# A graph network's tensor product: when the second 0/1 tile and the second turned row of a two-block group are made

## The reference

```python
w = _mlp(emb, fc1_w1, fc1_w2)                 # per edge: 512 weights from 10 numbers
s_t = a1 * (einsum(s1, Wss) + einsum(vdot1, Wvv))
v_t = a1 * (einsum(s1, Wsv) * sh1 + einsum(v1, Wvs))
w2 = _mlp(emb, fc2_w1, fc2_w2)
scal, gates, vecs = ...                       # second product, of s_t and v_t in the same way
edge_out = concatenate([tanh(scal), vecs * tanh(gates)]) * norm
return segment_sum(edge_out, edge_dst, num_segments=12500)
```

## Time and profile before

| | |
|---|---|
| median of 3 runs | 30745.3 us (30692.2 to 30746.5) |
| profiled execution | 30631.3 us, span 30629.5 us |
| busy, whole span | PE 82%, PEld 53%, DVE 59%, ACT 15%, POOL 55% |
| tensor-product stage | from about 21011 us to 30600 us |
| its costliest VectorE groups | L1763 2308.7 us, L1755 2050.7 us |
| its costliest TensorE groups | L1894 3515.9 us, L1882 2122.7 us |

### The profile page before, as it was taken

How to read it: one execution, slowest core, us unless ns; L and a number is a source line. 1 busy time by engine, 2 the same in 40 slices (tenths; PEclk the granted TensorE clock), 3 DMA queues, 4 the chain that set the end, 5 groups by cost and what they waited for, 6 DMA issues and landing times. The chain is left out here.

```text
span 30629.5 us, 606961 instructions
## 1 busy us (share of the span) xinstructions
PE 25062.6 (82%) x149627; PEld 16349.8 (53%) x149628; DVE 18026.0 (59%) x47075; ACT 4486.4 (15%) x12240; POOL 16710.3 (55%) x16857
## 2 busy tenths in 40 slices
PE   8777776666669888876999997666888888888888
PEld 6444443222238888854767675663444444444444
DVE  9211114666663333334666666886777777777777
ACT  4111111111110000001111111221111111111111
POOL 0677776777767777734777775552333333333332
PEclk9555555555555555555566666997999999999999
DMA  2111112222221111103333336552222222222222
GB/s 65 35 30 30 30 30 47 51 51 51 51 44 25 25 25 25 25 13 54 79 80 79 79 79 90 172 171 68 70 70 70 70 71 71 71 69 70 69 70 64
DMA packets 2615643, 1869.03 MB, mean 61 GB/s; under 512 B 1600555, under 2 KB 2081065, under 8 KB 2613814
## 3 DMA queue, kind: packets, MB, share of 16 engines
q1 hardware_dynamic: 1914438, 1424.41, 17.5%
q0 software_dynamic: 516000, 217.22, 5.7%
q10 hardware_dynamic: 184400, 220.54, 2.9%
HBM read 1621.01 MB, written 238.82 MB: 61 GB/s over the span
## 5 line engine op out<-in xcount | busy, mean ns | idle before, releaser
L2030 POOL DMA_INDIRECT rows_x<-x_table,index x3125 | 3031.6, 970 | 6787.0 <-DMA index<-in_src 6025.1
L1295 POOL DMA_INDIRECT rows<-x_table,index x3625 | 3456.8, 954 | 1997.6 <-issue 1237.4
L162 PE MATMUL banks<-rows,onehot 128*128 128x33 f32 (+1 forms) x14440 | 3416.8, 413 | 1062.1 <-issue 601.7
L547 POOL DMA_INDIRECT rows<-x_table,index x3125 | 3026.0, 968 | 1852.1 <-issue 939.7
L162 PEld LDWEIGHTS banks<-rows,onehot 128*128 128x128 f32 x14440 | 3185.9, 328 | 1370.0 <-issue 1360.8
L905 POOL DMA_INDIRECT bucket_pairs<-pair,place_int x3125 | 3145.7, 1007 | 1275.2 <-issue 1213.5
L696 POOL DMA_INDIRECT rows<-x_table,index x3125 | 3108.0, 995 | 1019.5 <-issue 951.7
L1894 PE MATMUL banks<-first,same_unit 128*128 128x384 f32 (+1 forms) x10000 | 3515.9, 478 | 0.0
L1205 DVE CUSTOM_DVE_ANT_0 junk<-banks,mask 128x320 f32<-128x320 f32 x5800 | 2550.5, 486 | 1546.4 <-PE banks L1240 1523.9
L1763 DVE TENSOR_TENSOR second<-banks,h 128x384 f32<-128x384 f32 (+1 forms) x5000 | 2308.7, 484 | 1093.8 <-PE banks L1894 1050.6
L1882 PE MATMUL banks<-u_turned,w_tensor 32*128 32x384 f32 (+1 forms) x10000 | 2122.7, 502 | 522.7 <-DVE first L1755 522.7
(11 more groups left out here) (396 smaller groups left out, 38439.1 us busy)
## 6 DMA issues: line engine op xcount, KB each, us to landing
key_row<-key_rows SPq DMA_DIRECT2D x1450, 320.0 KB
h<-hidden_dram SPq DMA_DIRECT2D x10000, 40.0 KB
key_row<-dst_rows SPq DMA_DIRECT2D x625, 320.0 KB
rows<-x_table,index POOLq DMA_INDIRECT x9875
a_dram<-a ACTq DMA_DIRECT2D x625, 160.0 KB
a<-a_dram SPq DMA_DIRECT2D x625, 160.0 KB
rows_dram<-rows ACTq DMA_DIRECT2D x725, 90.0 KB
x_rows<-rows_dram SPq DMA_DIRECT2D x725, 90.0 KB
```

The source lines that it names most:

```text
L162: mm = nc.tensor.matmul(m["ps"][7][:, 0:width], m["onehot"][j % 3][:, t * P:(t + 1) * P], rows[:, t, :], start=t == 0, stop=t == T - 1)
L547: nc.gpsimd.indirect_dma_start(out=m["rows"][j][:, t * W:t * W + F], out_offset=None, in_=m["x_table"], in_offset=bass.IndirectOffsetOnAxi ...
L1295: nc.gpsimd.indirect_dma_start(out=m["rows"][j][:, t * XA:t * XA + F], out_offset=None, in_=m["x_table"], in_offset=bass.IndirectOffsetOnA ...
L2030: nc.gpsimd.indirect_dma_start(out=m["rows_x"][j][:, t * F:(t + 1) * F], out_offset=None, in_=m["x_table"], in_offset=bass.IndirectOffsetO ...
```

## The change

Three things move, and only for two-block groups do products and tiles themselves come in another order:

- On VectorE the first add of g-3 goes from behind the gates to between `first` quarter 1 and the front (`dve_first_visit`). It now waits for `returned` of group g-2 too. With two blocks, the second 0/1 tile is made right behind it. The second add stays where the visits were (`dve_further_visits`).
- The second turned row is made without a loop around it; the wait until TensorE has used it and the memset L1818 go behind `second` quarter 1 (`dve_turned_last`), which reads the group's word once more.
- The words are read at the start of VectorE's turn, since the first add needs a block number. On TensorE, further visits wait for `first_added` and `summed_up` and step a counter first.

A loop over third and later visits stays in the code for groups with more than two blocks, of which there are none.

```diff
-            with dve.Fori(1, visits) as k:
+            nc.vector.tensor_scalar(m["hot_turned"][:, :], m["key_row"][j][:, :], m["part_at"][:, 1:2], None, ALU.is_equal).then_inc(s["more_turned"], 1)
+
+    def dve_turned_last(dve, i, j, n):
+
+        with dve.If(n > 1):
+            _, visits, further = window_of(nc, dve, m, s, SLOTS * i + j)
+            with dve.If(visits > 2), dve.Fori(2, visits) as k:
                 dve.wait_ge(s["more_owned"], ONE + further + k - 1)
...
+    def dve_first_visit(dve, i, j, first, n):
+        g = SLOTS * i + j
+
+        if not (isinstance(i, int) and g == GROUPS - 1):
+            dve.wait_ge(s["returned"], ONE + g + 2)
         dve.wait_ge(s["first_summed"], ONE + g + 1)
-        add(sums_at(0), first).then_inc(s["first_added"], 1)
+        dve_add(sums_at(0), first).then_inc(s["first_added"], 1)
+        with dve.If(n > 1):
+            hot(g, j, 1).then_inc(s["more_hot"], 1)
+
+    def dve_further_visits(dve, i, j, n):
...
+            with dve.If(visits > 2), dve.Fori(2, visits) as k:
+                dve.wait_ge(s["summed"], ONE + further + k - 1)
+                add(sums_at(1), block_of_visit(k - 1)).then_inc(s["added"], 1)
                 hot(g, j, k).then_inc(s["more_hot"], 1)
-                dve.wait_ge(s["summed"], ONE + further + k)
-                add(sums_at(1), to).then_inc(s["added"], 1)
+            dve.wait_ge(s["summed"], ONE + further + visits - 1)
+            add(sums_at(1), block_of_visit(visits - 1)).then_inc(s["added"], 1)

     def dve_turn(dve, i, j):
+        if there(i, j, -3) or there(i, j, 2):
+            first, n, _, n_ahead = turn_words(dve, i, j)
         if there(i, j, 0):
             dve_first(dve, i, j, 0)
         if there(i, j, -1):
             dve_second(dve, *at(i, j, -1), 2)
         if there(i, j, 0):
             dve_first(dve, i, j, 1)
+        if there(i, j, -3):
+            dve_first_visit(dve, *at(i, j, -3), first, n)
         if there(i, j, 1):
             dve_front(dve, *at(i, j, 1))
         if there(i, j, -1):
             dve_second(dve, *at(i, j, -1), 3)
-        if there(i, j, -3) or there(i, j, 2):
-            first, n, _, n_ahead = turn_words(dve, i, j)
...
         if there(i, j, -3):
-            dve_visits(dve, *at(i, j, -3), first, n)
+            dve_further_visits(dve, *at(i, j, -3), n)
...
             dve_second(dve, i, j, 1)
+        if there(i, j, 2):
+            dve_turned_last(dve, *at(i, j, 2), n_ahead)
...
     def pe_further_visits(pe, i, j, n):
         with pe.If(n > 1):
             _, visits, further = window_of(nc, pe, m, s, SLOTS * i + j)
+            pe.wait_ge(s["first_added"], ONE + SLOTS * i + j + 1)
+            if not (isinstance(i, int) and SLOTS * i + j == GROUPS - 1):
+                pe.wait_ge(s["summed_up"], ONE + SLOTS * i + j + 2)
+            pe.sem_inc(s["going"], 1)
```

More of the change, by code:

```diff
@@ L1818, in dve_turned_further, with dve_add @@
         nc.vector.memset(m["done"][:, :], 0.0).then_inc(s["rows_owned"][j], 1)
-    def dve_visits(dve, i, j, first, n):
+    def dve_add(sums, to):
+        block = m["acc"][:, bass.ds(to * W, W)]
+        return nc.vector.tensor_tensor(block, block, sums, ALU.add)
+    def dve_first_visit(dve, i, j, first, n):
         g = SLOTS * i + j
-        def add(sums, to):
-            block = m["acc"][:, bass.ds(to * W, W)]
-            return nc.vector.tensor_tensor(block, block, sums, ALU.add)
+        if not (isinstance(i, int) and g == GROUPS - 1):
+            dve.wait_ge(s["returned"], ONE + g + 2)
         dve.wait_ge(s["first_summed"], ONE + g + 1)
-        add(sums_at(0), first).then_inc(s["first_added"], 1)
+        dve_add(sums_at(0), first).then_inc(s["first_added"], 1)
[3 more added lines that the diff above has]
+        g = SLOTS * i + j
+        add = dve_add
         with dve.If(n > 1):
             begin, visits, further = window_of(nc, dve, m, s, g)
-            with dve.Fori(1, visits) as k:
-                to = nc.s_assert_within(begin + k, 0, NB - 1, skip_runtime_bounds_check_because="first + n <= NB")
+            block_of_visit = lambda k: nc.s_assert_within(begin + k, 0, NB - 1, skip_runtime_bounds_check_because="first + n <= NB")
+            with dve.If(visits > 2), dve.Fori(2, visits) as k:
+                dve.wait_ge(s["summed"], ONE + further + k - 1)
+                add(sums_at(1), block_of_visit(k - 1)).then_inc(s["added"], 1)
                 hot(g, j, k).then_inc(s["more_hot"], 1)
-                dve.wait_ge(s["summed"], ONE + further + k)
-                add(sums_at(1), to).then_inc(s["added"], 1)
+            dve.wait_ge(s["summed"], ONE + further + visits - 1)
+            add(sums_at(1), block_of_visit(visits - 1)).then_inc(s["added"], 1)
     def dve_turn(dve, i, j):
+        if there(i, j, -3) or there(i, j, 2):
+            first, n, _, n_ahead = turn_words(dve, i, j)
         if there(i, j, 0):
@@ L2056, in _ @@
             dve_turned_further(dve, 0, 0, n)
+            dve_turned_last(dve, 0, 0, n)
             dve_turn(dve, -1, SLOTS - 1)
```

## The result

The changed kernel takes 30582.96 us (30579.53 to 30610.34, 5 runs), the kernel before, beside it, 30744.42 us: ratio 0.9954 [0.9939, 0.9968], 161 us or 0.46% faster. The forecast was 0.4% slower; the time lies inside the range, near the rival "Faster", on the other side of no change.

The account below looks back on a forecast made before the run. TensorE was taken to set the pace of the tensor-product stage, waiting by name for VectorE. Terms -495 + 148 + 283 + 53 + 39 + 97 = +125 us on the 30745.3 us median gave 30870 us, 0.4% slower; range 30480 to 31240.

Parts of the forecast that it names:

- Faster: Lone TensorE idle spell behind the jump costs no clock: (c) zero, (e) without clock term; 30490 us, chance 0.28.
- (a): Second turned row, 97 turns: 1.1 us saved there, 4.0 us behind as the clock holds; -495 us.
- (b): Words and new block uncovered at the loop's jump: 0.8 and 0.4 us at 123 jumps, +148 us.
- (c): Behind the jump TensorE idles 1.95 us; clock falls at 105 jumps, 2.7 us each, +283 us.
- (d): First add between L1755 and L1740 costs 0.1 us in each of 528 plain turns, +53 us.
- (e): Second visit, 97 turns: early tile lengthens the stretch before the transposes, +39 us; clock falls sooner, +97 us.
- The skip that refetches: Skips crossing the held code cost up to 2.8 us once an iteration, 350 us; 31220 us, chance 0.08.

Follow-up runs that it names:

- e7: Changed kernel with the words read behind quarter 0 of first and dve_turned_last ahead of dve_second(..., 1); 30417.87 us, ratio 0.9908 to the kernel before.
- f4: Kernel before with only the second turned row made ahead, its block between first quarter 3 and second quarter 1; 30420.14 us, ratio 0.9911.
- f1: Kernel before with only the second turned row made ahead, its new block at the turn's end, before the jump; 30673.46 us, ratio 0.999.
- e8: Changed kernel with the second 0/1 tile made late, behind the gates as before; 30578.25 us, ratio 0.9954 to the kernel before.
- c3: The changed kernel run again, nothing altered, as yardstick; 30578.19 us, ratio 0.9953 to the kernel before.
- f3: Kernel before with only the reading of the words moved to the start of VectorE's turn; 30724.37 us, ratio 1.0014.

## Why the prediction was wrong, point by point

**(a) Second turned row: right in kind, a quarter too large.** The wait is gone, L1755 follows at once, TensorE's spell is 0.47 us, and the turns behind fell 29 times of 97 instead of 93 and went from 16.36 to 13.86 us on average (forecast 13.2). The turned-row turns themselves gave the 1.1 us of the step. The 4.0 us for the turn behind were read from one turn: over all 97 it was 2.9 us longer than plain turns of its slot before the change, so more could not come back, and 2.5 did. With the turned-row turns themselves the two rows give -348 us, in e7 without the jump's cost -377, in f4 alone -344, where the step had -495. It also took the clock as always saved; it still fell in three turns in ten.

**(b) Words and block at the jump: right.** TensorE's spell grew by 1.3 us where the step had 1.2, VectorE's idle time in the turn of the earlier trace rows from 1.88 to 3.09. Of its parts the words cost 0.9 us (forecast 0.8), the block 0.3 us (forecast 0.4); in f1, where skip and jump take longer, the block costs 0.9. The traces show 122 jumps; the forecast's 123 counts one wait at the end of the stage too.

**(c) The clock behind the jump: the step that failed.** The mechanism is as written: 46 of the 57 plain first turns behind a jump fell, none before. The price was not: a fallen turn takes 1.6 us more than one that held (13.83 against 12.22), where the step took 2.7. Nor was the count of jumps that pay. Against e7 the jumps' slots cost 241 us, of which the idle spell is (2.03 - 0.88) x 122 = 140; about 100 are left for the clock, where the term was 283. Of the 100 the plain turns are 46 x 1.6 = 74. The other 65 first turns, those near a two-block group, are together only 23 us longer: 52 of them had fallen in the kernel before already (28 in e7, 56 in the changed kernel), where the step took off some 18.

**(d) The add: the delay right, its cost not to be told from nothing.** L1740 stands 0.97 us behind the start of L1755 where it stood 0.87 us: 0.10 us. Slots 1 to 3 of the plain turns changed by 11 us in 176 turns, slot 3 even got shorter (13.19 to 12.91 us), which the step did not foresee; scaled to the step's 528 groups they are 33 us. But f1 and f4, which leave the add where it was, show +11 and +24 us in the same turns, so the sum's 53 us are neither confirmed nor refuted.

**(e) Second visit: wrong in size, +136 forecast, about +34 measured.** Visit turns went from 19.33 to 19.69 us; e8 shows that the tile has no part in it. The step counted the clock's earlier fall and the longer stretch before the transposes; it gave the earlier products no gain, where their saved wait (1.77 to 0.98 us) pays for the later transposes (0.41 to 1.21). The turns behind the visits are another 38 us longer, 16 in e7.

**The sum and the rivals.** With (a) as in e7, (b) as forecast and the others as measured: -377 + 148 + 100 + 33 + 34 = -62 us; the stage shows -109, the medians -161, so some 50 to 100 us are in none of the steps. Of the 47 us to the stage, 38 are slots 1 to 3, which are shorter in the changed kernel than in e7 (c3: 9 us); the 52 us from there to the medians may be the low execution that was profiled before. Correcting (c) and (e) alone takes +125 to -160, (c) being the larger of the two; that this is the measured -161 is luck, since the error of (a) goes the other way. The rival "Faster" had nearly the right time with the wrong mechanism: the clock does fall behind the jump, it only costs less.

**The skip that refetches** didn't come at its price of 2.8 us: the new block's skip takes 0.23 us in four slots of the changed kernel and 0.55 us in slot 1. Milder, something like it is there: in f1 the skip in front of the jump takes 0.53 us and the jump 0.4 us more than in f4.

**Range and chances.** The range held the time by its low end. What weighed falsely was a price of 2.7 us taken from the earlier trace rows, from a turn that pays for low clock over a whole turn of TensorE-bound work, for turns where the earlier trace rows shows VectorE alone on the path for half of the time.

## What to carry to other kernels

Nothing should stand at a loop's jump that can stand a step later: there 0.9 us of register work went on the path whole and could cost the clock too, and two moved blocks were worth more (0.5%) than the change had left. Price a fall of the clock from a turn with the same bound as the one where it will happen, and count it only where the clock is still up. An early operand is worth its wait only if the consumer's own sequencer is ready, and only if what it is put in front of is not on the path.

## What the runs showed of the hardware

- With one idle spell of TensorE of 1.69 us (median, f3) the clock fell in 5 of 57 turns, with 1.85 us (f1) in 37 of 57, with 0.93 us or less in none; within f1 the spells of fallen and held turns are of the same length.
- A fall behind the jump cost 1.6 to 2.0 us in a turn of 12.2 us, with 6 to 7 us of it at 1.2 GHz on average.
- The loop's jump back leaves VectorE without an instruction for 2.8 to 3.3 us (medians of 122 in the kernels here). A skipped block took 0.23 us in most slots and 0.5 to 0.6 us in some, nearly the same in every iteration.
- Reading the word behind the jump (f3) cost 0.92 us, a skipped block ahead of it 0.9 us in f1 and 0.3 us in the changed kernel.
- The same kernel took 30.7 ms on some chips and 36.3 ms on two others; there the clock fell in 25 of the 57 plain first turns without any change, where it fell in none on the first, and the change was worth 0.73% instead of 0.46%.
